# Attention pipeline of an attention and Mamba kernel: eleven-stage order, k's softmax in four exponentials, heads in two banks

## The chip, the cores and the metric

The kernel runs on one core of a Trainium2 chip. The metric is the device time of one execution in microseconds (us), and lower is better. The engines are TensorE (PE, its weight loads are listed apart as PEld), VectorE (DVE), ScalarE (ACT), GpSimd (POOL) and the DMA queues, here issued by SyncE (SP) and by ScalarE.

## What is computed

`x` has 128 sequences of 64 steps and 256 features. A first layer normalises x, makes q, k and v, and does a linear attention with 16 heads of 16 features:

```python
xn = layernorm(x);  q, k, v = xn @ Wq + bq, xn @ Wk + bk, xn @ Wv + bv
k = where(mask, -inf, k);  v = where(mask, 0, v)
q = softmax(q, over the 16 features of a head);  k = softmax(k, over the 64 steps)
attn = einsum('bhse,bhsd->bhed', k, v);  y = einsum('bhtd,bhed->bhte', q, attn)
scale, shift = split(silu(emb) @ film_emb_W + film_emb_b)
x = x + silu(layernorm(y) * (1 + scale) + shift) @ film_out_W + film_out_b
```

A second layer normalises that again, modulates it with the rows of `silu(c) @ W_ada + b_ada`, runs a Mamba scan over the 64 steps and adds the result, gated. `c` and `emb` are the same input `cond`.

## The kernel before

There are two phases, one after the other. **The attention phase** works on 64 tiles of 128 tokens (two sequences of 64 steps in each). It is a software pipeline written out by hand. Every engine has a function `iteration(j, stages)`, which `attention_iterations` calls for j = 0 to 70; work under `if s in stages` is for tile j - s. An engine issues its work strictly in the order of the code, so the order inside `iteration` is the schedule. Between engines there are counting semaphores: `later(eng, S["name"], k)` waits until tile k's step has been done, and `reuse(eng, S["name"], k, slots)` waits until a buffer with so many slots has come free. **The Mamba phase** (`mamba_*`) begins on every engine with `attention_over`, which waits for the last stores of the attention phase. It starts with a gather from the tensor `normed`.

One tile goes through these steps, with the profile's line numbers: VectorE's statistics of x (L1533, L1540), GpSimd's reciprocal root (`rstd`, L1184, L1186), VectorE's normalising (`xn`, L1579), TensorE's turning (L1301), ScalarE's scale and bias out of the bank (`xnT`, L1391), TensorE's products for k (L1283) and for q and v (L1293). VectorE adds bias and mask to k (L1567), takes the maximum over the 64 steps (L1589), subtracts it (L1605), ScalarE takes the exponential of 128x256 at once (L1398), VectorE adds up (L1556) and inverts (L1561), and GpSimd multiplies (L1194). q goes through bias (L1602), maximum (L1608), subtraction (L1617), exponential (L1407), sum (L1553) and reciprocal (L1558). TensorE turns k and q (L1321, L1324), ScalarE copies them (L1403). `heads_product` (L1264) multiplies k by v with 64 rows of the array for each of the two sequences, both into the bank `b_at`; its second half waits for `at_half`, the end of the first, and the product for k (L1283) stands between the halves. VectorE masks the heads (L1584), TensorE makes y (L1311), VectorE scales it (L1612) and takes its statistics; GpSimd normalises it (`yn`, L1174), TensorE turns it (L1345), ScalarE applies four scale and bias columns (L1423) and a tanh (L1427), VectorE finishes the activation (`fs`, L1595), TensorE makes the output product (L1335), VectorE adds x (L1624). x had the output bias added by GpSimd (L1218). GpSimd normalises the sum (`xh`, L1174) and SyncE stores `resid` and `normed`. Further GpSimd work for each tile is the mask row as numbers (`mneg`, L1210).

Once-only work stands at the end of certain iterations: conditioning, film products (L1246, j = 3), and the ada products (L1253 and L1255, at j = 4 and 5 on TensorE into `b_fo_ps`), which VectorE turns into modulation rows (L1518) and a gate row (L1528).

Of the kernel before, what the change touches and what calls it, by code (L numbers as in the profile page):

```python
# [54 lines left out]
STAGES = 8  # L55
# [8 lines left out]
def build(nc, x, cond, itok, mask, norm_scale, norm_bias, Wq, bq, Wk, bk, Wv, bv,  # L64
# [6 lines left out]
    ssm_out = nc.dram_tensor("ssm_out", (BATCH, STEPS, D), F32, kind="Internal").ap()  # L71
    resid_seq = resid.rearrange("(b t) f -> b t f", t=STEPS)
    normed_seq = normed.rearrange("(b t) f -> b t f", t=STEPS)

    with ExitStack() as ctx:  # L75
# [52 lines left out]
        mask_bc = sb("mask_bc", [P, MRING, P], attn_mem, I32)  # L128
# [13 lines left out]
        kmax = sb("kmax", [P, FB * SEQS], attn_mem)  # L142
        ksum = sb("ksum", [P, FB * SEQS], attn_mem)
# [20 lines left out]
        for par in range(2):  # L164
# [17 lines left out]
        bank = [ctx.enter_context(nc.psum_tensor(f"bank{i}", [P, 512], F32)) for i in range(8)]  # L182
        b_xT, b_qvp, b_kT, b_kq, b_at, b_y, b_ynT, b_fo_ps = bank
# [22 lines left out]
        s_mask_f = sem("mask_as_float")  # L206
        s_mask_turned = sem("mask_turned")
# [9 lines left out]
        names = ("x_stats x_meanvar x_rstd x_norm xT_ready xnT_ready qv_ready kT_ready mneg_ready "  # L217
                 "k_biased k_max k_shifted k_exp k_sum k_rec k_normed q_max q_shifted q_exp q_sum q_rec v_ready "
                 "kq_turned kq_ready at_half at_ready at_masked y_ready y_scaled y_stats y_meanvar y_rstd y_norm ynT_ready "
# [17 lines left out]
        def reuse(eng, s, tile, slots):  # L237

            if tile >= slots:
                eng.wait_ge(s, tile + (1 - slots))  # L240

# [849 lines left out]
        def _(sp):  # L1091
            def load(k):

                reuse(sp, S["x1_ready"], k, XRING)
                apart(sp)
                sp.dma_start(xt[:, k % XRING, :], x_tok[k * P:(k + 1) * P, :]).then_inc(s_x[k % XRING], 16)
                reuse(sp, S["mneg_ready"], k, MRING)
                apart(sp)
                sp.dma_start(mask_bc[:, k % MRING, :],
                             mask_flat[k * P:(k + 1) * P].rearrange("(a n) -> a n", a=1).to_broadcast([P, P]))\  # L1100
                    .then_inc(s_mk[k % MRING], 16)
# [24 lines left out]
            weights(s_fo_w, (w_fo[:, :, :], film_out_W))  # L1126
            columns(s_cols_b, (fb_col, film_b), (fns_col, film_norm_scale), (fnb_col, film_norm_bias),
                    (conv_bias, conv_b), (dt_bias, b_dt), (d_col, D_param))

            def iteration(j, stages):  # L1130
                if j > 0 and j + AHEAD < TILES:
                    load(j + AHEAD)
                if 7 in stages:
                    k = j - 7
# [3 lines left out]
                if 6 in stages:  # L1138
                    k = j - 6
# [16 lines left out]
        def _(gp):  # L1156
# [20 lines left out]
            def iteration(j, stages):  # L1177
                done = [n for n, stage in enumerate((1, 5, 7)) if stage in stages]
                if done:
                    p, n = (j - 1) % 2, slice(done[0], done[-1] + 1)  # L1180
                    for norm in done:
                        later(gp, S[("x_meanvar", "y_meanvar", "x1_meanvar")[norm]], j - (1, 5, 7)[norm])
                    apart(gp)
                    gp.tensor_scalar(rstd[:, n, p, 1:2], mv[:, n, p, 1:2], EPS, None, ALU.add).then_inc(S["var_plus"], 1)  # L1184
                    later(gp, S["var_plus"], j - 1)
                    gp.tensor_tensor(rstd[:, n, p, 0:1], rstd[:, n, p, 1:2],  # L1186
                                     half_pow[:, None, :].to_broadcast([P, len(done), 1]), ALU.pow)\
                        .then_inc(S["rstd_ready"], 1)
                    later(gp, S["rstd_ready"], j - 1)
# [6 lines left out]
                if 5 in stages:  # L1196
                    k = j - 5
                    reuse(gp, S["ynT_ready"], k, 1)
                    apart(gp)
                    normalise(yn[:, :], yt[:, :], 1, k % 2, "y_norm")  # L1200
                if 7 in stages:
                    k = j - 7
                    gp.wait_ge(s_xh_out[k % 2], 16 * (k // 2) + 16)
                    apart(gp)
                    normalise(xh[:, k % 2, :], x1[:, k % 2, :], 2, k % 2, "xh_ready")
                if 0 in stages:
                    gp.wait_ge(s_mk[j % MRING], 16 * (j // MRING) + 16)
                    reuse(gp, S["k_biased"], j, MRING)
                    apart(gp)
                    gp.tensor_scalar(mneg[:, j % MRING, :], mask_bc[:, j % MRING, :], 1.0, -1e30,  # L1210
                                     ALU.is_equal, ALU.mult).then_inc(S["mneg_ready"], 1)
                if 2 in stages:
# [5 lines left out]
                    gp.tensor_tensor(x, x, b_fo[:, :], ALU.add).then_inc(S["x_biased"], 1)  # L1218

# [5 lines left out]
        def _(pe):  # L1225
# [14 lines left out]
            def film_products():  # L1240

                pe.wait_ge(s_condT, 1)
                pe.wait_ge(s_film_in, 16)
                for m in range(4):
                    for c in range(KC):
                        mm = pe.matmul(b_ynT[:, m * P:(m + 1) * P], film_w[:, c, m * P:(m + 1) * P], cond_T[:, c, :],  # L1246
# [3 lines left out]
            def ada_products(a, b):  # L1250

                dst = b_fo_ps[:, 0:b - a]
# [7 lines left out]
            def heads_product(k, q):  # L1260

                rows = slice(q * STEPS, (q + 1) * STEPS)
                for h in range(FB):
                    mm = pe.matmul(b_at[:, (q * FB + h) * P:(q * FB + h + 1) * P], vt[rows, k % 4, h * P:(h + 1) * P],  # L1264
# [3 lines left out]
            def iteration(j, stages):  # L1268
                if 4 in stages:
# [4 lines left out]
                    heads_product(k, 0).then_inc(S["at_half"], 1)  # L1274
# [14 lines left out]
                if 2 in stages:  # L1289
                    k = j - 2  # L1290
                    reuse(pe, S["qv_biased"], k, 1)
                    for c in range(FB):
                        mm = pe.matmul(b_qvp[:, :], xnT[:, k % 2, c, :], w_qv[:, c, :],  # L1293
                                       start=(c == 0), stop=(c == FB - 1))
                    mm.then_inc(S["qv_ready"], 1)
                if 1 in stages:
                    k = j - 1
                    later(pe, S["x_norm"], k)
                    reuse(pe, S["xnT_ready"], k, 1)
                    for c in range(FB):  # L1300
                        mm = pe.transpose(b_xT[:, c * P:(c + 1) * P], xn[:, c * P:(c + 1) * P], ident[:, :])  # L1301
                    mm.then_inc(S["xT_ready"], 1)
                if 4 in stages:
                    k = j - 4
                    later(pe, S["at_masked"], k)
                    reuse(pe, S["y_scaled"], k, 1)
                    if k == 0:
                        pe.wait_ge(s_condT, 1)
                    for i in range(4):
# [37 lines left out]
                if j == 1:  # L1347
                    turn_mask()
# [337 lines left out]
```

## Time and profile before

| | |
|---|---|
| runs | 2012.58 us median of 3 (2011.74 to 2015.48) |
| profiled execution, its own time | 2011.82 us |
| its span, first to last instruction | 2010.1 us |
| busy share of the span | PE 94%, DVE 94%, POOL 85%, ACT 82%, PEld 73% |
| attention phase | from the start to 488.2 us, when the last tile's store of `normed` is issued |

In the lists of instructions in order of time a row gives the start in us from the span's start, the length in us, the engine, the line, the operation, output and inputs, the shape and how many instructions it merges. In brackets stands the idle time before it and who ended it. Neighbours on one engine overlap a little, so the distance from start to start is what an instruction costs its engine, and it is less than its length.

### The profile page before, as it was taken

To read this page: it belongs to the slowest core of one execution; us is meant where nothing else is said; L and a number is where in the kernel's file an instruction comes from. 1 tells how busy PE (TensorE), PEld (TensorE's weight loads), DVE (VectorE), ACT (ScalarE), POOL (GpSimd) and SP (SyncE) were. 2 spreads that over 40 slices of the span, in tenths; PEclk is the share of its full clock that TensorE was granted. 3 is DMA by queue.
4 is the path that set the end of the run, shared out by engine and by line. 5 is a ranking of instruction groups with operands and counts; after the bars stand their busy time and mean duration, and the time that the engine had idled before them with its cause. 6 is when DMAs were issued, how large, how long until landed. Compare 5 with 4: busy or idle time off the path is not lost. (4 is left out here: it accounts for less than half of the span.)

```text
span 2010.1 us, 42901 instructions
## 1 busy us (share of the span) xinstructions
PE 1881.6 (94%) x12641; PEld 1463.5 (73%) x12641; DVE 1897.2 (94%) x3750; ACT 1648.6 (82%) x3563; POOL 1701.6 (85%) x1929
## 2 busy tenths in 40 slices
PE   6999999995799999999999999999999999999873
PEld 4666666663378787787878778787878788787773
DVE  5999999995699999999999999999999999999997
ACT  2555655563799999999999999999999999999881
POOL 3788888887289999999999999999999999998582
PEclk9999999997999999999999999999999999999997
DMA  6222222211000000000000000000000000001164
GB/s 169 62 66 65 70 69 66 65 61 58 26 7 11 17 12 12 12 13 11 17 17 12 12 12 12 12 17 6 17 17 12 12 12 12 12 7 48 59 226 183
DMA packets 71401, 80.78 MB, mean 40 GB/s; under 512 B 12227, under 2 KB 63619, under 8 KB 69124
## 3 DMA queue, kind: packets, MB, share of 16 engines
q1 hardware_dynamic: 69024, 70.67, 11.3%
q10 hardware_dynamic: 2148, 7.38, 1.0%
q8 instruction: 105, 1.72, 0.4%
q14 instruction: 124, 1.02, 0.2%
HBM read 44.46 MB, written 33.55 MB: 39 GB/s over the span
## 5 line engine op out<-in xcount | busy, mean ns | idle before, releaser
L814 ACT ACTIVATE decay<-dtT,decay_rate 128x256 f32<-128x256 f32 x2048 | 864.8, 495 | 0.6
L690 PE MATMUL bank<-ident,decay 128*128 128x128 f32 x4096 | 612.9, 273 | 46.5 <-DVE state L951 23.3
L690 PEld LDWEIGHTS bank<-ident,decay 128*128 128x128 f32 x4096 | 477.6, 142 | 105.3 <-ACT decay L814 63.7
L705 PEld LDWEIGHTS bank<-ident,scaled 128*128 128x128 f32 x3496 | 414.5, 141 | 180.9 <-issue 145.7
L705 PE MATMUL bank<-ident,scaled 128*128 128x128 f32 x3496 | 529.1, 274 | 1.9 <-POOL scaled L598 0.2
L951 DVE SCALAR_TENSOR_TENSOR fresh<-dtx,bc,bank 128x512 f32<-128x512 f32 x512 | 357.7, 740 | 0.0
L951 DVE SCALAR_TENSOR_TENSOR state<-dtx,bc,bank 128x512 f32<-128x512 f32 x512 | 357.6, 740 | 0.0
L941 DVE TENSOR_TENSOR bank<-bank,state 128x512 f32<-128x512 f32 x512 | 338.0, 693 | 19.7 <-PE bank L690 14.8
L941 DVE TENSOR_TENSOR bank<-bank,fresh 128x512 f32<-128x512 f32 x512 | 336.4, 692 | 14.0 <-PE bank L690 9.3
L598 POOL TENSOR_SCALAR scaled<-state,bc 128x512 f32<-128x512 f32 x378 | 261.7, 699 | 70.4 <-DVE state L951 44.8
L598 POOL TENSOR_SCALAR scaled<-fresh,bc 128x512 f32<-128x512 f32 x381 | 265.2, 699 | 39.7 <-DVE fresh L951 27.3
L622 POOL TENSOR_TENSOR xs<-xs,tap_bcT 128x512 f32<-128x512 f32 x174 | 222.7, 1280 | 13.4
L603 POOL TENSOR_TENSOR scaled<-scaled 128x512 f32<-128x512 f32 x150 | 192.3, 1282 | 2.5
L1391 ACT ACTIVATE xnT<-bank,col 128x128 f32<-128x128 f32 x128 | 51.7, 454 | 156.5 <-PE bank L1301 156.5
L618 POOL TENSOR_SCALAR tap_bcT<-raw,taps 128x512 f32<-128x512 f32 x174 | 121.7, 699 | 25.6 <-DVE xs L1047 25.2
L1293 PE MATMUL bank<-w_qv,xnT 128*128 128x512 f32 x256 | 127.8, 622 | 0.0
L735 PE MATMUL bank<-w_out,zs 128*128 128x256 f32 x512 | 126.2, 380 | 1.4 <-DVE zs L960 0.9
L747 PE MATMUL bank<-hT,w_in 128*128 128x512 f32 x240 | 122.3, 595 | 1.8 <-ACT hT L825 1.3
L738 PE MATMUL bank<-hT,w_in 128*128 128x512 f32 x240 | 122.9, 594 | 0.0
L860 ACT ACTIVATE scaled<-state,bc 128x512 f32<-128x512 f32 x134 | 95.5, 713 | 24.9 <-DVE state L951 24.8
L860 ACT ACTIVATE scaled<-fresh,bc 128x512 f32<-128x512 f32 x131 | 93.2, 711 | 12.6 <-DVE fresh L951 12.2
L735 PEld LDWEIGHTS bank<-w_out,zs 128*128 128x128 f32 x512 | 89.9, 190 | 10.2 <-issue 1.1
(164 smaller groups left out, 3269.8 us busy)
## 6 DMA issues: line engine op xcount, KB each, us to landing
xt<-in_x_dram SPq DMA_DIRECT2D x64, 128.0 KB, 2.3
resid<-x SPq DMA_DIRECT2D x64, 128.0 KB, 1.7
normed<-xh SPq DMA_DIRECT2D x64, 128.0 KB, 1.7
fin_r<-resid SPq DMA_DIRECT2D x8, 1024.0 KB, 4.9
xg<-normed SPq DMA_DIRECT2D x60, 128.0 KB, 2.1
ssm_out<-yo SPq DMA_DIRECT2D x30, 256.0 KB, 2.1
tap_bcT<-ssm_out SPq DMA_DIRECT2D x44, 128.0 KB, 2.2
mask_bc<-in_mask_BxS_ik_dram SPq DMA_DIRECT2D x64, 64.0 KB, 2.9
```

The source lines that it names most:

```text
L598: gp.tensor_scalar(dst, h, cn, 1.0, ALU.mult, ALU.mult).then_inc(s_scaled_p, 1)
L603: gp.tensor_tensor(scaled[:, i % RING, :], scaled[:, i % RING, :], scaled[:, (i - 1) % RING, :], ALU.add)\
L622: gp.tensor_tensor(x, x, tap[:, :], ALU.add).then_inc(s_tapadd, 1)
L690: mm = pe.transpose(dec_bank[i % DECAY_BANKS][:, m * P:(m + 1) * P], decay[:, i // BLOCK % 2, n % GROUP, m, t % HALF * P:(t % HALF + 1) * ...
L705: mm = pe.matmul(y_bank[t % HALF][:, m * P:(m + 1) * P], scaled[:, i % RING, m * P:(m + 1) * P], ident[:, :], is_transpose=True, start=Fal ...
L735: mm = pe.matmul(side[:, q * D:(q + 1) * D], zs[k % 2][:, m, t * P:(t + 1) * P], w_out[:, m, :], start=(m == 0), stop=(m == CB - 1))
L738: mm = pe.matmul(side[:, :], w_in[:, piece, DI + b * P:DI + (b + 1) * P], hidden(k)[:, piece, :], start=(piece == 0), stop=(piece == FB - 1))
L814: act.activation(decay[:, block % 2, e // CB, m, :], dtT[c % 2][:, m, half * HTOK:(half + 1) * HTOK], ACT.Exp, scale=decay_rate[:, m, n:n ...
L860: act.activation(dst, h, ACT.Copy, scale=cn).then_inc(s_scaled_a, 1)
L941: ve.tensor_tensor(dec_bank[i % DECAY_BANKS][:, :], dec_bank[i % DECAY_BANKS][:, :], h, ALU.mult)\
L951: ve.scalar_tensor_tensor(state_of(n, t), dtx[c % 2][:, t, :], bc[:, c % 2, t, n:n + 1], dec_bank[i % DECAY_BANKS][:, :], ALU.mult, ALU.ad ...
L1293: mm = pe.matmul(b_qvp[:, :], xnT[:, k % 2, c, :], w_qv[:, c, :], start=(c == 0), stop=(c == FB - 1))
```

## The change

The attention pipeline is reordered and regrouped:

- Eleven stages instead of eight. The numbers are now counted apart for each engine: VectorE starts with tile j at j and ends it at j + 6, TensorE uses stages 2 to 7, ScalarE 0 to 4, GpSimd 1 to 9, SyncE up to 10. The order of work in every `iteration` is new.
- k's softmax: VectorE gives the negative maximum. ScalarE takes four exponentials of 128x64, each with the negative maximum as its bias and with a sum as a further output (`accum_out`). VectorE's subtraction and sum of k are gone.
- The two halves of `heads_product` go into two banks (4 and 5) and are issued one behind the other, with no semaphore between them. VectorE masks both in one instruction.
- The turned x and the turned y share one bank (`b_turn`), with waits so that TensorE doesn't write while ScalarE reads.
- The mask as numbers is made once by VectorE, stored to DRAM by ScalarE's queue, and loaded for each tile by broadcast into `mneg`. GpSimd's work on it is gone.
- The ada products move to the end: TensorE's iteration 68, into `b_qvp` and `b_kT`, and VectorE's rows of them to its iteration 67. Film products go into `b_fo_ps`, an iteration later for TensorE.

The diff, cut to its core:

```diff
-STAGES = 8
+STAGES = 11
+X_STAGE, Y_STAGE, X1_STAGE = 1, 5, 8
...
+        low, heads, high = [ps(f"bank{i}", 512) for i in range(4)], ps("bank45", 1024), [ps(f"bank{i}", 512) for i in (6, 7)]
+        b_turn, b_qvp, b_kT, b_kq, _, _, b_y, b_fo_ps = bank
+        b_xT, b_ynT = b_turn[:, 0:D], b_turn[:, D:2 * D]
+        b_at = heads[:, :].rearrange("p (q f) -> p q f", q=SEQS)[:, :, 0:2 * P]
...
         # sync
+            def load_mask(k):
+                reuse(sp, S["k_biased"], k, MRING)
+                sp.dma_start(mneg[:, k % MRING, :], mask_rows[k:k + 1, :].to_broadcast([P, P])).then_inc(s_mk[k % MRING], 16)
+            sp.wait_ge(s_mask_out, 16)
+            for k in range(AHEAD + 1):
+                load_mask(k)
...
         # gpsimd: xh of j-9, k's product of j-3, x's bias of j-2, then rstd for (j-1, j-5, j-8), then yn of j-5
-                if 0 in stages:
-                    gp.tensor_scalar(mneg[:, j % MRING, :], mask_bc[:, j % MRING, :], 1.0, -1e30,
-                                     ALU.is_equal, ALU.mult).then_inc(S["mneg_ready"], 1)
...
         # tensor: q,v product of j-3; turn k,q of j-4; y of j-5; turn y of j-6; turn x of j-2; output of j-7;
         #         both heads products of j-4; k product of j-2
-                    heads_product(k, 0).then_inc(S["at_half"], 1)
+                    heads_product(k, 0)
+                    heads_product(k, 1).then_inc(S["at_ready"], 1)
-                if 4 in stages:
-                    later(pe, S["at_half"], j - 4)
-                    heads_product(j - 4, 1).then_inc(S["at_ready"], 1)
+                if j == TILES + 4:
+                    later(pe, S["qv_biased"], TILES - 1)
+                    ada_products(b_qvp[:, :], 0, 2 * D)
+                    later(pe, S["k_biased"], TILES - 1)
+                    ada_products(b_kT[:, 0:D], 2 * D, 3 * D)
...
         # scalar: exp of q and v of j-2; exp of k of j-1; copy k,q of j-2; xnT of j; film of j-4
+            act.wait_ge(s_mask_f, 2)
+            act.dma_start(mask_rows, mask_row[:, :]).then_inc(s_mask_out, 16)
-                    act.activation(kk, kk, ACT.Exp).then_inc(S["k_exp"], 1)
+                    later(act, S["k_max"], k)
+                    for g in range(FB * SEQS):
+                        kk = kT[:, k % 2, g, :]
+                        ins = act.activation(kk, kk, ACT.Exp, bias=kmax_neg[:, g:g + 1],
+                                             accum_out=ksum[:, k % 2, g:g + 1])
+                    ins.then_inc(S["k_exp"], 1)
...
         # vector: stats of x j; mean of y j-4; shift q j-2; mean of x j; x1 of j-6; bias k j-1; mask heads j-3;
         #         max k j-1; fs j-5; xn j; stats of x1 j-6; sum q j-2; bias qv j-1; 1/sum q j-2; scale y j-3;
         #         max q j-1; 1/sum k j-1; stats of y j-3; mean of x1 j-6
-                    ve.tensor_reduce(ksum[:, :], kT[:, k3 % 2, :, :], AX.X, ALU.add).then_inc(S["k_sum"], 1)
-                    ve.tensor_tensor(kk, kk, kmax[:, :, None].to_broadcast([P, FB * SEQS, STEPS]), ALU.subtract)\
-                        .then_inc(S["k_shifted"], 1)
+                    ve.tensor_reduce(kmax_neg[:, :], kT[:, k1 % 2, :, :], AX.X, ALU.max, negate=True)\
+                        .then_inc(S["k_max"], 1)
-                if j == 4:
-                    clamp_order()
-                    modulation_rows()
-                if j == 5:
-                    mamba_constants()
-                    gate_rows()
+                if j == 6:
+                    clamp_order()
+                if j == 7:
+                    mamba_constants()
+                if j == TILES + 3:
+                    modulation_rows()
+                    gate_rows()
```

The lines that begin with `#` sum up the new order of an engine in words; they are not in the kernel.

## Rows read from the trace of the kernel before

**Rows 1.** The page's first part: busy time and share of each engine.

```profile
PE 1881.6 (94%) x12641; PEld 1463.5 (73%) x12641; DVE 1897.2 (94%) x3750; ACT 1648.6 (82%) x3563; POOL 1701.6 (85%) x1929
```

**Rows 2.** Busy time by stretch: steady part and tail (after the bounds, PE to POOL).

```profile
51.07:454.46 403.39, 396.68 (x2322) 274.86 (x2321) 396.26 (x1276) 239.04 (x638) 328.07 (x405) 1.00 0.22 66
454.46:488.50 34.04, 22.43 (x120) 14.52 (x118) 21.20 (x61) 13.16 (x36) 23.85 (x29) 0.82 0.14 47
```

**Rows 3.** Waits from 100 to 450 us: sum, times, longest.

```profile
PEld bank L1264 <- ACT kq L1403: 17.8, 50, 0.5
```

**Rows 4.** Instructions in order of time: VectorE in one steady iteration.

```profile
251.29 0.41 DVE L1556 TENSOR_REDUCE ksum<-kT 128x4 f32<-128x256 f32 x1
...
251.62 0.24 DVE L1558 RECIPROCAL qrec<-qsum 128x16 f32<-128x16 f32 x1
...
251.85 0.61 DVE L1567 SCALAR_TENSOR_TENSOR kT<-bank,col,mneg 128x128 f32<-128x128 f32 x2
...
252.37 0.42 DVE L1533 BATCH_NORM_STATS2 stats<-xt 128x6 f32<-128x256 f32 x1
...
252.72 0.66 DVE L1579 TENSOR_SCALAR xn<-xt,mv,rstd 128x256 f32<-128x256 f32 x1
...
253.30 0.68 DVE L1584 TENSOR_TENSOR attnT<-bank,head_mask 128x512 f32<-128x512 f32 x1
...
253.90 0.40 DVE L1589 TENSOR_REDUCE kmax<-kT 128x4 f32<-128x256 f32 x1
...
255.22 0.41 DVE L1605 TENSOR_TENSOR kT<-kT,kmax 128x256 f32<-128x256 f32 x1
```

**Rows 5.** In order of time: GpSimd's two-tensor work in that iteration.

```profile
252.62 0.61 POOL L1194 TENSOR_TENSOR kT<-kT,krec 128x256 f32<-128x256 f32 x1
...
256.62 0.73 POOL L1218 TENSOR_TENSOR xt<-xt,b_fo 128x256 f32<-128x256 f32 x1
```

**Rows 6.** In order of time: two encounters of GpSimd and VectorE, at 51 and 464 us.

```profile
50.53 1.23 POOL L1174 TENSOR_SCALAR yn<-yt,mv,rstd 128x256 f32<-128x256 f32 x1
...
51.07 0.40 DVE L1579 TENSOR_SCALAR xn<-xt,mv,rstd 128x256 f32<-128x256 f32 x1
...
464.12 0.73 POOL L1218 TENSOR_TENSOR xt<-xt,b_fo 128x256 f32<-128x256 f32 x1
...
464.35 0.79 DVE L1617 TENSOR_TENSOR qe<-qv,qmax 128x256 f32<-128x256 f32 x1
```

**Rows 7.** In order of time: TensorE and ScalarE groups of the steady iteration.

```profile
250.44 1.27 ACT L1423 ACTIVATE fu<-bank,film_t,film_s 128x64 f32<-128x64 f32 x4
...
254.18 0.66 PE L1311 MATMUL bank<-attnT,kq 128*64 128x128 f32 x8
...
254.28 0.81 ACT L1391 ACTIVATE xnT<-bank,col 128x128 f32<-128x128 f32 x2 [2.12 <-PE bank L1301]
...
255.99 0.58 ACT L1403 ACTIVATE kq<-bank 128x512 f32<-128x512 f32 x1
...
256.62 0.71 PE L1264 MATMUL bank<-kq,vt 64*128 64x128 f32 x4
...
257.26 1.16 PE L1283 MATMUL bank<-xnT,w_k 128*128 128x128 f32 x8
```

**Rows 8.** In order of time: landmarks of the fill, the ada products and the tail.

```profile
17.16 0.61 DVE L1567 SCALAR_TENSOR_TENSOR kT<-bank,col,mneg 128x128 f32<-128x128 f32 x2 [2.58 <-PE bank L1283]
...
35.25 1.12 PE L1253 MATMUL bank<-b_mod,ones_row 1*128 1x512 f32 x2
...
40.04 0.42 DVE L1518 SCALAR_TENSOR_TENSOR mod_scale<-bank,gamma_bc 128x256 f32<-128x256 f32 x1 [1.98 <-PE bank L1255]
...
57.26 0.61 DVE L1567 SCALAR_TENSOR_TENSOR kT<-bank,col,mneg 128x128 f32<-128x128 f32 x2
...
460.62 0.61 DVE L1567 SCALAR_TENSOR_TENSOR kT<-bank,col,mneg 128x128 f32<-128x128 f32 x2
...
488.20 0.34 SPq L1137 DMA_DIRECT2D normed<-xh  x1
```

More of the change, by code:

```diff
@@ L1268, in iteration @@
             def iteration(j, stages):
+                if 3 in stages:
+                    k = j - 3
+                    if k == 0:
+                        pe.wait_ge(s_attn_w, 16 * 5)
+                    later(pe, S["xnT_ready"], k)
+                    reuse(pe, S["qv_biased"], k, 1)
+                    for c in range(FB):
+                        mm = pe.matmul(b_qvp[:, :], xnT[:, k % 2, c, :], w_qv[:, c, :],
+                                       start=(c == 0), stop=(c == FB - 1))
+                    mm.then_inc(S["qv_ready"], 1)
@@ new lines, in iteration @@
+                if 5 in stages:
+                    k = j - 5
+                    later(pe, S["at_masked"], k)
+                    reuse(pe, S["y_scaled"], k, 1)
+                    if k == 0:
+                        pe.wait_ge(s_condT, 1)
+                    for i in range(4):
+                        q, h = i // FB, i % FB
+                        mm = pe.matmul(b_y[q * STEPS:(q + 1) * STEPS, h * P:(h + 1) * P],
+                                       kq[:, k % 2, D + h * P + q * STEPS:D + h * P + (q + 1) * STEPS],
+                                       attnT[:, i, :], start=True, stop=True)
+                    mm.then_inc(S["y_ready"], 1)
@@ new lines, in iteration @@
+                if 2 in stages or 6 in stages:
+                    kx, ky = j - 2, j - 6
+                    if 0 < kx <= TILES:
+                        later(pe, S["xnT_ready"], kx - 1)
+                    if 0 < ky <= TILES:
+                        later(pe, S["film_in"], ky - 1)
+                if 6 in stages:
+                    later(pe, S["y_norm"], ky)
+                    for c in range(FB):
+                        mm = pe.transpose(b_ynT[:, c * P:(c + 1) * P], yn[:, c * P:(c + 1) * P], ident[:, :])
+                    mm.then_inc(S["ynT_ready"], 1)
@@ L1296, in iteration @@
[L1296 to L1309, printed above, removed]
-                        q, h = i // FB, i % FB
-                        mm = pe.matmul(b_y[q * STEPS:(q + 1) * STEPS, h * P:(h + 1) * P],
-                                       kq[:, k % 2, D + h * P + q * STEPS:D + h * P + (q + 1) * STEPS],
-                                       attnT[:, i, :], start=True, stop=True)
-                    mm.then_inc(S["y_ready"], 1)
@@ L1338, in iteration @@
[L1338 to L1347 removed]
+                if j == 2:
```

358 lines of the change are left out of this document (170 added, 188 removed).

## The prediction, made before the result was known

> **What bounds the kernel now.** I read the page's busy shares first [rows 1]: PE and DVE stand equal at 94%, so the average decides nothing. The change touches the attention phase alone, so next I read the busy time by stretch. Between VectorE's normalising of tile 5 (51.07 us) and of tile 63 (454.46 us) the loop is steady: 58 periods in 403.39 us, 6.95 us each, with VectorE busy 396.26 us and TensorE 396.68 us, both 98% [rows 2]. Busy time of PE includes waits inside a matmul's record, so the third view is the list of waits: in 100 to 450 us VectorE has none worth a row, while TensorE's loads wait 0.35 us in each of 50 iterations for ScalarE's copy of k and q, which in turn comes behind VectorE's chain [rows 3]. VectorE's queue is full and sets the period; TensorE is a few tenths behind. The fourth view, instructions in order of time, prices each step from start to start [rows 4 to 8].
>
> **VectorE's period.** Gone are the sum of k, 0.33 us from start to start (251.29 to 251.62), and the subtraction, of the same length 0.41 us, so 0.33 us too [rows 4]. The negated maximum I cost like the maximum, 0.40 us long as before, the same shape. That leaves 6.95 - 0.66 = 6.29 us.
>
> Two encounters with GpSimd move. Today xn lasts 0.66 us (0.58 from start to start), because k's product on GpSimd (two tensors) begins at 252.62, just before it [rows 4, 5]. At 51.07 the same xn lasts 0.40 us though GpSimd's yn has been running since 50.53 [rows 6]. So GpSimd's tensor by tensor work holds up such a VectorE instruction and its scalar work doesn't. In the new order xn comes while GpSimd does yn, so xn costs 0.40 less the usual overlap of 0.08, 0.32 us: 0.26 us less. But k's reciprocal now starts GpSimd's k product, and then x_biased: 0.61 + 0.73 us plus about 0.08 us ahead of each, so x_biased runs from 0.77 to 1.50 us after the reciprocal's end. VectorE meanwhile does two statistics (0.35 each, as 252.37 to 252.72 [rows 4]) and two means (tiny tensors, an estimate of 0.1 each), and comes to q's subtraction, with two tensors in SBUF, about 0.9 us after it. It is caught. The row for that is at 464.35: the same q subtraction, with x_biased on GpSimd since 464.12, took 0.79 us and ended 0.29 us after it [rows 6]. So it ends at 1.79 instead of 1.31: 0.45 us more. VectorE's period: 6.29 - 0.26 + 0.45 = 6.48 us. Bounds: 6.03 us if the two miss each other, 6.55 us if both collisions stay.
>
> The Trainium skill (SBUF — State Buffer, Who interferes with whom) says more: a two-tensor DVE instruction contends with any GpSimd instruction that reads SBUF, and a DVE instruction in a two-port mode and GpSimd block each other for the whole instruction. The trace agrees for 464.35 and disagrees for 51.07, where xn began amid yn and was not held.
>
> **TensorE's period.** Today four heads matmul passes (one half) last 0.71 us and there are two such groups, while y's eight passes in two column halves need 0.66 us together [rows 7], so the column halves run side by side. In two banks the row halves may do so too: one group of some 0.66 instead of 2 x 0.64 us from start to start (256.62 to 257.26), 0.64 us less. One interruption of the full-width products goes as well: k's product takes 1.16 us for eight passes of 128 columns between the halves, against 0.66 for eight in pairs. So 6.95 less 0.64 is at most 6.3 us, and about 6.1 with a further switch saved. If the halves don't overlap, 0.45 us comes back, 6.55 to 6.75 us. I take 6.1 to 6.3: hidden behind VectorE.
>
> The Trainium skill (TensorEngine Tiling (Array Packing), Gotcha 1: PSUM Pressure) says that row tiles write different banks and can't use one bank at once; no row of this trace has row halves in two banks, so it can't be checked yet.
>
> **The four exponentials.** Four activations of 64 columns with column operands take 1.27 us (fu) [rows 7]. The sum's read-out, x us for each, has no row. Below: 0. Above: a whole small activation's slot, 1.27/4 = 0.3 us. I take half, 0.15. ScalarE was busy 239.04/58 = 4.1 us a period [rows 2]; with 1.27 + 0.6 on top, and the single exponential not even taken off, it is 6.0, so its sum is no bound. Its place in the order can be: the loop kmax 0.40, four exponentials 1.27 + 4x, copy of k and q 0.50, xnT 0.81, k's product 1.16 [rows 7], k's bias 0.52 (251.85 to 252.37), masking of heads 0.60 (253.30 to 253.90) [rows 4], and some 0.16 for four handovers. Sum 5.42 + 4x: 6.0 us at 0.15, 6.6 us at 0.3. So at 0.15 it lies hidden behind 6.48; it sets the period from x = 0.27 on.
>
> **GpSimd and the DMAs.** GpSimd loses the mask work (0.66 us in 5.66, 328.07/58 [rows 2]) and stays under the period. SyncE issues the same number of DMAs for a tile. Its queue now waits once for the mask's round trip through DRAM, behind which stand the columns for film; and load_mask(j + 2) waits for VectorE's bias of tile j - 2, with two whole iterations before the data are needed. I cost these at nothing; if the first masks are late, the first k bias moves by 1 to 3 us.
>
> **Steady part.** From k's bias of tile 5 (57.26) to that of tile 63 (460.62) it is 403.4 us [rows 8]. After: 58 x 6.48 = 375.8, and 2.3 us (an estimate, about a dozen short instructions of 0.2) for order table and Mamba constants, which now fall there: 378.1. Gain 25.3 us.
>
> **Fill.** The first k bias was at 17.16, the sixth at 57.26 [rows 8]: 40.1 us. The first x no longer waits behind the second tile's load, so I put the first bias at about 15, 2.1 us earlier (it can't be before k's weights have landed). Out of the 40.1 go the wait for the ada products 1.98 [rows 8], the four modulation instructions (like mod_scale, 0.35 each, 1.4 us), and the 2.3 us just moved: 34.4; the film products stay. The gate's wait and the k work that five filling iterations no longer do (0.66 each, where VectorE doesn't wait anyway) give about another 1.4: 33. Gain 2.1 + 7.1 = 9.2 us, bounds 5 and 12.
>
> **Tail.** From 460.62 to the last store of normed at 488.20: 27.6 us [rows 8]. TensorE waits a lot there and its granted clock is 0.82 on average over 454 to 488 us, i.e. part of it at 1.2 GHz [rows 2]. The ada products now stand there: 4.8 us for the first 512 columns (35.25 to 40.04) [rows 8], half of it for the other 256, 7.2 us together. They stand ahead of the turn of the last y, which TensorE could otherwise do after some 3 us of that wait, so 4.4 us are exposed. Without them I get 21 us for the last tile's chain (k softmax 3.4, k product and turning 2.9, copy and heads 1.4, masking and y 1.5, statistics 1.2, root and yn 2.4, turn and film 2.4, fs, output, x1 and mean 2.8, root, xh and store 2.9). So 25.4 us, gain 2.2 us; bounds 6.6 gained (all hidden) and 0.7 lost (all exposed). They keep TensorE busy, so its clock should not fall before they end.
>
> **Sum.** 25.3 + 9.2 + 2.2 = 36.7 us. The Mamba phase behind 488.2 us starts from the same gather and is unchanged. The profiled execution took 2011.82, the median is 2012.58: 2012.6 - 36.7 = 1975.9, say 1976 us. Own range: period 6.3 to 6.6 and fill and tail bounds, 1960 to 1988.
>
> **Rivals.**
> 1. *The q subtraction misses x_biased.* For it: the margin is only some tenths. Then VectorE needs 6.03 and TensorE's 6.1 to 6.3 sets the period, at 6.2: 58 x 0.28 = 16 us less, 1960 us.
> 2. *GpSimd's yn holds up xn and fs after all, or the heads don't overlap.* xn would wait for yn's end, about 0.3 us in each iteration, period 6.8; serial heads give 6.55 to 6.75. Against the first: the row at 51.07. Time 1976 + 58 x 0.3 = 1993 us. By the skill's rule named above (SBUF — State Buffer), it is what would come out.
> 3. *The exponentials become the bound, slower than before.* Place: ScalarE between kmax and the copy of k and q. If the read-out waits for each activation's end and then takes a full slot, x is near 0.5, and 5.42 + 2.0 = 7.4 us; against before it decides from x = 0.38 (6.95 us). Time 1976 + 58 x 0.94 = 2031 us. Against: the nearest row has four small activations in 1.27 us, so it would have to more than double them.
> 4. *The gain dissolves in new waits* (the longer way of a tile through more stages doesn't pay in the tail, the period stays at 6.9): 2000 to 2012 us. Against: VectorE's queue is full today and two instructions leave it.
>
> **How the numbers follow.** Forecast 0.50, rival 1 0.17, rival 2 0.16, rival 3 0.08, rival 4 0.09 (a third of it within 0.2% of before). From no change this measurement tells about 0.2%, 4 us. Faster: 0.50 + 0.17 + 0.16 + 0.05 = 0.88; same 0.03; slower 0.08 + 0.01 = 0.09. The range takes in rivals 1 and 2 with their spread: 1953 to 1998 us. Out of it lie rivals 3 and 4 and the far end of rival 1.
>
> **What would show it.** Right: a period of VectorE near 6.5 us with 98% busy and no waits; xn at 0.40 us and q's subtraction at 0.8; heads passes in pairs within 0.7 us; the exponentials at 1.3 to 2 us for four; ada products between 430 and 450 us. Wrong: a row in which VectorE waits for TensorE's k product or for heads (ScalarE's chain too long), xn above 0.6 (rival 2), q's subtraction at 0.41 (rival 1), or a fill whose first k bias waits for a mask.

## The result and the profile after

The changed kernel takes 1984.71 us (1982.53 to 1986.35), against 2012.57 us (2011.74 to 2015.48) for the kernel before: ratio 0.9857, 95% interval 0.9845 to 0.9868. That is 28 us less, where 36.7 were forecast; the time lies 9 us above the forecast and inside its range of 1953 to 1998 us. The profiled execution took 1983.11 us, its span 1979.6 us.

First part of the page, of the changed kernel, for [rows 1]:

```profile
PE 1828.8 (92%) x12641; PEld 1424.4 (72%) x12641; DVE 1841.2 (93%) x3623; ACT 1706.3 (86%) x4011; POOL 1659.6 (84%) x1867
```

The landmarks of [rows 8], sixth k bias to last k bias, from there to the last store of `normed`, and the Mamba phase; busy time by stretch, changed kernel:

```profile
52.51:431.28 378.77, 348.79 (x2321) 238.46 (x2320) 347.09 (x1169) 291.50 (x1045) 294.30 (x348) 1.00 0.22 69
431.28:459.77 28.49, 19.24 (x100) 11.29 (x98) 16.46 (x49) 10.49 (x34) 19.77 (x25) 0.94 0.19 61
459.77:1979.50 1519.73, 1426.24 (x10024) 1150.70 (x10024) 1449.25 (x2314) 1381.69 (x2856) 1326.31 (x1458) 0.99 0.09 29
```

The account against the landmarks of before [rows 8]: fill 57.26 to 52.51, 4.8 us less; steady part 403.36 to 378.77, 24.6 us less (6.53 us a period instead of 6.95); tail 27.6 to 28.5, 0.9 us more. Together 28.4 us. The Mamba phase went from 1521.9 to 1519.8 us; in the runs below with the same Mamba phase it is anywhere from 1519 to 1521 us, so I count that as spread.

Two of the 58 periods, the first two, took 8.04 and 7.87 us: the order table and the Mamba constants now fall there. The other 56 have a mean of 6.48 us, exactly the period that was forecast.

The steady figure looks like a hit (25.3 forecast), but the row says something else: VectorE is busy 347 of 379 us, 92%, where I had said 98% and no waits. The waits of the changed kernel, 100 to 430 us (some 50 iterations; sum, times, longest), rows that matter:

```profile
POOL xh L1194 <- issue: 50.9, 47, 1.7
...
PE bank L1327 <- POOL yn L1194: 25.9, 50, 1.2
...
DVE kT L1597 <- PE bank L1360: 22.8, 42, 0.8
```

And those of SyncE's queue in that stretch:

```profile
SPq L240 <- DVE kT L1597: 216.6, 48, 5.1
```

Before, in the same stretch:

```profile
SPq L231 <- POOL xh L1174: 195.6, 48, 4.7
```

SyncE then waited for GpSimd's `xh`, that is for the work that it was to store. Now it stands in `load_mask`, waiting for VectorE's k bias, for 4.5 us in each of 48 iterations. What lies behind that in its queue is seen in order of time, changed kernel, steady part:

```profile
250.00 0.61 DVE L1597 SCALAR_TENSOR_TENSOR kT<-bank,col,mneg 128x128 f32<-128x128 f32 x2 [0.72 <-PE bank L1360]
...
250.70 0.32 SPq L1117 DMA_DIRECT2D mneg<-mask_rows  x1
...
251.13 0.37 SPq L1157 DMA_DIRECT2D normed<-xh  x1
251.33 1.48 POOL L1194 TENSOR_SCALAR yn<-yt,mv,rstd 128x256 f32<-128x256 f32 x1 [0.24 <-POOL rstd L1225]
...
251.79 0.49 DVE L1621 TENSOR_SCALAR xn<-xt,mv,rstd 128x256 f32<-128x256 f32 x1
...
252.25 0.33 ACT L1419 ACTIVATE kT<-kT,kmax_neg 128x64 f32<-128x64 f32 x1
252.49 0.19 ACT L1419 ACTIVATION_READ_ACCUMULATOR kT<-kT,kmax_neg 128x1 f32 x1
252.58 0.33 ACT L1419 ACTIVATE kT<-kT,kmax_neg 128x64 f32<-128x64 f32 x1
...
254.06 1.22 POOL L1194 TENSOR_SCALAR xh<-x,mv,rstd 128x256 f32<-128x256 f32 x1 [1.26 <-issue]
...
255.08 0.38 DVE L1580 TENSOR_TENSOR qe<-qv,qmax 128x256 f32<-128x256 f32 x1
...
255.25 0.69 POOL L1208 TENSOR_TENSOR kT<-kT,krec 128x256 f32<-128x256 f32 x1
...
258.04 1.40 POOL L1194 TENSOR_SCALAR yn<-yt,mv,rstd 128x256 f32<-128x256 f32 x1 [0.24 <-POOL rstd L1225]
...
259.58 0.41 PE L1327 MATMUL bank<-ident,yn 128*128 128x128 f32 x2 [0.64 <-POOL yn L1194]
...
261.00 0.72 PE L1279 MATMUL bank<-kq,vt 64*128 64x128 f32 x8
...
262.86 0.61 DVE L1597 SCALAR_TENSOR_TENSOR kT<-bank,col,mneg 128x128 f32<-128x128 f32 x2 [0.71 <-PE bank L1360]
```

Read it as one loop. The k bias (250.00 to 250.61) lets the mask load go (250.70), and only behind that stands the store of `normed` (251.13). Such a store takes 2.8 us to land (median), and GpSimd's next `xh` needs the landing of a store, since there are two `xh` buffers; it begins 1.26 us late here (254.06). The profile names no releaser for that wait ("issue"); that it is the store is read from the code and from 251.13 + 2.8 = 253.9, and tested with e1 and e6. It makes GpSimd late with k's product, x's bias, `rstd` and `yn` (258.04). TensorE stands 0.64 us before the turn of y (259.58), behind which are queued the heads (261.00) and the product for k, and for that VectorE's k bias waits 0.71 us (262.86). Two iterations, 12.9 us.

Three things are also to be seen here. The exponentials start 0.33 us apart, and the read of the sum (0.19 us) lies almost wholly under its neighbours. The eight heads passes, both halves, need 0.72 us. And q's subtraction lasts 0.38 us.

### The profile page after: what moved, and what is told of

Read it like the earlier page. It is cut to its first block and busy times, and to the rows that moved or that the text cites. A ratio compares the mean times of both kernels' runs of the same rounds, so it can differ in the third digit from the quotient of the medians.

```text
span 1979.6 us, 43161 instructions
## 1 busy us (share of the span) xinstructions
PE 1828.8 (92%) x12641; PEld 1424.4 (72%) x12641; DVE 1841.2 (93%) x3623; ACT 1706.3 (86%) x4011; POOL 1659.6 (84%) x1867
## 3 DMA queue, kind: packets, MB, share of 16 engines
q14 instruction: 125, 1.02, 0.2%
## 5 line engine op out<-in xcount | busy, mean ns | idle before, releaser
L1419 ACT ACTIVATE kT<-kT,kmax_neg 128x64 f32<-128x64 f32 x256 | 85.8, 336 | 74.5 <-DVE kmax_neg L1610 74.5
L633 POOL TENSOR_SCALAR tap_bcT<-raw,taps 128x512 f32<-128x512 f32 x174 | 120.9, 695 | 25.0 <-DVE xs L1062 24.6
L1194 POOL TENSOR_SCALAR xh<-x,mv,rstd 128x256 f32<-128x256 f32 x64 | 78.4, 1225 | 57.2 <-issue 55.1
L1291 PE MATMUL bank<-w_qv,xnT 128*128 128x512 f32 x256 | 122.5, 601 | 0.0
L1194 POOL TENSOR_SCALAR yn<-yt,mv,rstd 128x256 f32<-128x256 f32 x64 | 90.7, 1417 | 15.2 <-POOL rstd L1225 15.2
```

The lines of the kernel that those rows point to most:

```text
L1194: gp.tensor_scalar(dst, src, mv[:, norm, slot, 0:1], rstd[:, norm, slot, 0:1], ALU.subtract, ALU.mult).then_inc(S[done], 1)
```

## Experiments

Each kernel below is the changed one with one or more edits, but for e8, which is the kernel before with one part of the change. Period is from the sixth to the last k bias, over 58. The kernel before was measured again beside each group of runs, with medians from 2010.85 to 2013.72 us, so differences of medians between kernels of different groups are good to some 3 us; the ratios allow for it. Where kernels are compared by a wait over 100 to 430 us, I use the mean without the first two periods: 6.48 us for the changed kernel, 6.25 in e1, 6.73 in e2, 6.72 in e11, 6.71 in e10.

| kernel | ratio to before, 95% | median, us | period | tail | first and sixth k bias |
|---|---|---|---|---|---|
| changed | 0.9857 (0.9845 to 0.9868) | 1984.71 | 6.53 | 28.5 | 18.47, 52.51 |
| e1, six mask buffers | 0.9795 (0.9778 to 0.9811) | 1970.78 | 6.30 | 28.5 | 19.06, 54.93 |
| e6, stores first | 0.9786 (0.9770 to 0.9803) | 1969.95 | 6.31 | 29.0 | 19.41, 53.56 |
| e7, e1 and x's bias last | 0.9773 (0.9756 to 0.9789) | 1966.94 | 6.25 | 28.5 | 18.93, 52.54 |
| e9, e7 and e5 | 0.9767 (0.9751 to 0.9784) | 1964.64 | 6.25 | 28.4 | 16.73, 52.66 |
| e5, ada weights late | 0.9859 (0.9842 to 0.9875) | 1982.93 | 6.59 | 29.0 | 16.95, 50.43 |
| e4, ada products last | 0.9870 (0.9854 to 0.9887) | 1986.78 | 6.56 | 25.4 | 18.70, 53.86 |
| e3, serial heads | 0.9999 (0.9986 to 1.0012) | 2011.75 | 6.95 | 28.4 | 19.11, 56.34 |
| e10, e1 and serial heads | 0.9946 (0.9926 to 0.9965) | 1999.22 | 6.74 | 28.4 | 18.94, 56.36 |
| e2, one exponential | 0.9950 (0.9933 to 0.9966) | 2001.91 | 6.79 | 29.3 | 17.77, 54.26 |
| e11, e1 and one exponential | 0.9947 (0.9931 to 0.9964) | 1999.31 | 6.78 | 29.3 | 18.46, 54.47 |
| e8, four exponentials in the kernel before | 1.0087 (1.0070 to 1.0104) | 2029.64 | 7.26 | 28.8 | 16.65, 57.40 |

### SyncE's queue: e1 and e6

e1:

```diff
-MRING = 4
+MRING = 6
```

> Changed kernel with six mask slots instead of four, nothing else. Theory Q (SyncE's queue): the steady period of 6.53 us is set by a loop over two iterations: VectorE's bias of k releases the mask load, behind which the store of xh stands in SyncE's queue; the store frees xh's buffer, GpSimd normalises into it, then does k's product, x's bias, the root and yn, and only then TensorE can turn y and x, make k's product, and the next but one bias follows (12.86 us from 250.00 to 262.86). With six slots the mask load waits for a bias two tiles older, so the store goes out early: GpSimd's xh has no wait, the period falls below 6.45 us, the time to 1955 to 1978 us. Since GpSimd then runs early, x_biased should meet q's subtraction, which takes 0.7 to 0.8 us instead of 0.39. Rival P (TensorE's k product comes late for its own reasons, ScalarE's exponentials first): no change, 1982 to 1987 us. Rival V (VectorE's own work is the bound): no change either.

e6 leaves the ring at four buffers and issues the mask's load behind the two stores:

```diff
                     load(j + AHEAD)
-                    load_mask(j + AHEAD)
                 if 10 in stages:
...
                     sp.dma_start(resid[k * P:(k + 1) * P, :], x1[:, k % 2, :]).then_inc(s_x1_out[k % 2], 16)
+                if j > 0 and j + AHEAD < TILES:
+                    load_mask(j + AHEAD)
```

> Changed kernel with four mask slots as it was, but in SyncE's iteration the mask load stands behind the two stores instead of ahead of them. Theory Q (the store stuck behind the mask load's wait is what costs): the same gain as with six slots, 1969 to 1973 us, and GpSimd's xh without the wait. Rival: six slots gained because masks arrived late at VectorE; then this edit, which makes them later still, gains nothing or loses, 1985 us or more.

Both take about 14 us off (13.9 and 14.8 by the medians, 12.5 and 14.3 by the ratios) and bring the period to 6.30. SyncE's queue of e1, 100 to 430 us:

```profile
SPq L240 <- DVE x L1589: 235.5, 54, 5.7
```

It now waits for nothing but VectorE's sum `x`, which the store of `resid` is to take, and GpSimd's wait before `xh` is gone from the list. Since e6 has the same gain with the old ring, it was not masks coming late but the stores standing behind a wait that isn't theirs.

One part of e1's expectation did not come. x's bias and q's subtraction do meet now, but VectorE isn't the one held:

```profile
250.55 1.03 POOL L1216 TENSOR_TENSOR xt<-xt,b_fo 128x256 f32<-128x256 f32 x1
250.60 0.39 DVE L1580 TENSOR_TENSOR qe<-qv,qmax 128x256 f32<-128x256 f32 x1
```

q's subtraction keeps its 0.39 us, where 0.7 to 0.8 were expected, and x's bias takes 1.03 instead of 0.73 us. More on it in the last section.

What is left at 6.30 is in e1's waits, 100 to 430 us:

```profile
POOL kT L1208 <- DVE krec L1650: 29.8, 28, 1.1
...
DVE kT L1597 <- PE bank L1360: 18.5, 26, 0.9
...
PE bank L1327 <- POOL yn L1194: 15.4, 27, 0.8
```

VectorE's and TensorE's come in every second iteration (start to start 5.94 and 6.54 us in turn). Without its wait VectorE would need 6.25 - 18.5/52.8 = 5.90 us, TensorE without its own 5.96: neither is full. That three engines hold each other in a loop is my reading of these waits, not shown by a run.

### GpSimd's order: e7

x's bias moves from before `rstd` to behind `yn` in GpSimd's iteration, on top of e1:

```diff
-                if 2 in stages:
...
-                    gp.tensor_tensor(x, x, b_fo[:, :], ALU.add).then_inc(S["x_biased"], 1)
...
                     normalise(yn[:, :], yt[:, :], 1, norm_slot(1, k), "y_norm")
+                if 2 in stages:
...
+                    gp.tensor_tensor(x, x, b_fo[:, :], ALU.add).then_inc(S["x_biased"], 1)
```

> Six mask slots, and GpSimd adds the output bias to x (x_biased) after yn instead of before the root. With six slots the periods alternate 5.94 and 6.54 us. Theory G: what is left is again a loop over two iterations, from VectorE's reciprocal of k through GpSimd's k product, x_biased (0.7 to 1.0 us), root and yn to TensorE's turns and k product; taking x_biased out of it makes it 0.7 to 1.0 us shorter for two iterations, and VectorE's own 5.94 us becomes the period: 58 x 0.36 = 21 us less than with six slots alone, 1950 us; at least 10 us less if q's subtraction now collides. Rival P (TensorE's sum with its copies from ScalarE is the bound): no change against six slots alone, 1969 to 1972 us.

It gives some 4 us at most (0.9773 against 0.9795, the intervals overlap), period 6.25, far from the 21 or at least 10 us of the first expectation. TensorE's wait for `yn` becomes rarer (20 instead of 27 times), but GpSimd then waits for VectorE's statistics. So GpSimd's length before `yn` is not what holds the loop at 6.3. What does is open.

### Heads in one or two waves: e3 and e10

Two banks as in the change, but the second half waits for the first:

```diff
-                    heads_product(k, 0)
+                    heads_product(k, 0).then_inc(S["at_half"], 1)
+                    later(pe, S["at_half"], k)
                     heads_product(k, 1).then_inc(S["at_ready"], 1)
```

> Changed kernel in which the second heads half waits for the end of the first, both in their own banks. The heads group becomes 0.65 us longer (0.43 us of passes and a drain). Theory Q: TensorE's heads stand in the two-iteration loop once, so a period gets 0.3 us longer: 12 to 20 us more, 1997 to 2005 us. Rival P: heads stand right ahead of k's product in each iteration, 0.65 us in each period, 38 us more, 2022 us. Rival V: no change.

The whole gain is gone: 27 us more than the changed kernel, period 6.95. That is between the two expectations (1997 to 2005 and 2022 us), and two readings were left: TensorE's own queue, or the loop through SyncE made longer. e10 is e3 with six mask buffers.

> Six mask buffers, and the second half of the heads waits for the end of the first (still two banks). Theory of the engine: the serial halves cost TensorE's own queue some 0.65 us an iteration, whatever the SyncE queue does; its sum of about 6.2 becomes 6.8 to 6.95, and the time is 2000 to 2010 us. Rival, theory of the loop: in the changed kernel the serial halves cost 27 us because they lengthened a loop that runs through the store and the mask's load; without that queue only a part comes back, period 6.4 to 6.6, 1977 to 1990 us.

1999 us, 28 us above e1: the engine, not the loop. TensorE and VectorE of e10 in order of time:

```profile
250.59 1.48 PE L1279 MATMUL bank<-kq,vt 64*128 64x128 f32 x8
...
251.44 1.03 POOL L1216 TENSOR_TENSOR xt<-xt,b_fo 128x256 f32<-128x256 f32 x1
251.48 0.39 DVE L1581 TENSOR_TENSOR qe<-qv,qmax 128x256 f32<-128x256 f32 x1
...
251.99 1.16 PE L1361 MATMUL bank<-xnT,w_k 128*128 128x128 f32 x8
...
253.19 0.61 DVE L1598 SCALAR_TENSOR_TENSOR kT<-bank,col,mneg 128x128 f32<-128x128 f32 x2 [0.91 <-PE bank L1361]
```

The same eight passes in the same two banks take 1.48 us instead of 0.72. In TensorE's list no wait on another engine is left, only its own 0.25 us between the halves, and VectorE waits 0.91 us for the product for k. So this kernel is bound by TensorE, at 6.7 us.

The Trainium skill (TensorEngine Tiling (Array Packing), Gotcha 1: PSUM Pressure) says that row tiles need different banks to run together. What can be seen here agrees: in two banks 0.72 us, in one bank [rows 7] two waves of 0.71. No run here let two row halves into one bank at once.

### k's softmax: e2, e11 and e8

e2 takes k's softmax back to one exponential with VectorE's subtraction and sum, in the new order:

```diff
...
-                    for g in range(FB * SEQS):
-                        kk = kT[:, k % 2, g, :]
-                        ins = act.activation(kk, kk, ACT.Exp, bias=kmax_neg[:, g:g + 1],
-                                             accum_out=ksum[:, k % 2, g:g + 1])
...
+                    act.activation(kk, kk, ACT.Exp).then_inc(S["k_exp"], 1)
...
         # vector
+                    ve.tensor_tensor(kk, kk, kmax_neg[:, :, None].to_broadcast([P, FB * SEQS, STEPS]), ALU.add)\
+                        .then_inc(S["k_shifted"], 1)
...
+                    ve.tensor_reduce(ksum[:, k1 % 2, :], kT[:, k1 % 2, :, :], AX.X, ALU.add).then_inc(S["k_sum"], 1)
```

> Changed kernel with k's softmax as before: subtraction and sum on VectorE, one exponential of 128x256 on ScalarE; order and banks as changed. Theory Q: VectorE has some 0.6 us of waiting in a period, so 0.66 us more work on it costs little: period 6.55 to 6.75, time 1985 to 1998 us. Rival V (VectorE bound): 58 x 0.66 = 38 us more, 2023 us. Rival P (the exponentials' chain is the bound): it gets faster, 1960 to 1980 us.

e11 is e2 with six mask buffers.

> Six mask buffers, and k's softmax as before (VectorE subtracts and adds up, ScalarE takes one exponential). Theory: with the store's wait gone VectorE's sum sets the period in both forms, so the two instructions of 0.33 us are paid in full: 6.30 + 0.66 = 6.96, but less the waits that VectorE still has at 6.30 (some 0.3), so 6.6 to 6.75 and 1988 to 1997 us. Rival: ScalarE's shorter way (one exponential instead of four) gives back more than half of it, period 6.45, 1980 us.

e2 costs 17 us over the changed kernel and e11 28 us over e1, both more than expected, with one and the same period, 6.79 and 6.78. In both VectorE's waits add up to 0.3 us at most from 100 to 430 us, so its own sum sets the period, 6.72 us without the first two. e1's 5.90 and 0.66 make 6.56. I put the remaining 0.16 down to collisions with GpSimd: in both the medians of `xn` and of q's subtraction are 0.56 and 0.59 us, against 0.41 and 0.39 in e1. That alone would be 0.35, so the sum doesn't close. With a full VectorE the queue of SyncE has no effect.

e8 is the same part of the change put alone into the kernel before.

> The kernel before with k's softmax alone changed (negated maximum, four exponentials with sums, no subtraction or sum on VectorE); eight stages, its order, its one heads bank. Theory: VectorE falls from 6.95 to 6.29 us a period, but TensorE, which waited only 0.35 us in a period, then sets it: period 6.6 to 6.9 us, time 1992 to 2009 us. Rival V (VectorE was the only bound, as the step in the prediction says): 6.3 us, 1975 us.

It makes that kernel slower, by 17 us, although two of VectorE's instructions leave; both expectations had it faster. Order of time, e8:

```profile
250.70 0.34 ACT L1400 ACTIVATE kT<-kT,kmax_neg 128x64 f32<-128x64 f32 x1
...
251.04 0.58 ACT L1407 ACTIVATE kq<-bank 128x512 f32<-128x512 f32 x1
251.06 0.42 DVE L1623 TENSOR_TENSOR x<-bank,xt 128x256 f32<-128x256 f32 x1 [0.42 <-PE bank L1335]
251.67 0.52 PEld L1264 LDWEIGHTS bank<-kq,vt 64*128 64x128 f32 x4 [0.67 <-ACT kq L1407]
251.67 0.71 PE L1264 MATMUL bank<-kq,vt 64*128 64x128 f32 x4 [0.43 <-ACT kq L1407]
...
253.50 0.61 DVE L1568 SCALAR_TENSOR_TENSOR kT<-bank,col,mneg 128x128 f32<-128x128 f32 x2 [0.34 <-PE bank L1283]
```

Four exponentials at 0.33 us stand ahead of the copy of k and q. TensorE's loads wait 0.67 us for that copy, where they waited 0.35 before [rows 3], and VectorE now waits for TensorE twice, 0.42 and 0.34 us. The period is 7.26 us.

No run has the new order with both the heads and the softmax as before, so what the order is worth by itself stays open.

### Start and end: e5, e9 and e4

e5 and e9 take the large `ada_w` load and three rows with it from the start to ScalarE's iteration 12:

```diff
...
+                if j == 12:
+                    load_ada_weights()
```

> Changed kernel in which the 1.5 MB of ada weights (with their bias, gamma and beta) are loaded at ScalarE's iteration 12 instead of 0. In the changed kernel the mask's store took 6.9 us to land, the first mask load went out at 12.71 and VectorE waited for it until 18.47 us, with the DMA engines full from 10 to 20 us. Theory: the weights' stream delays mask store and load; without it the first k bias comes at about 15 us and the time falls by 3 to 4 us, 1981 us. Rival: the delay is the queue of first weights (1 MB for q, k, v, output) and the order in SyncE's queue, so the first k bias stays past 17.5 us and the time at 1984 to 1986 us.

> The changed kernel with three edits together: six mask buffers, x's output bias last in GpSimd's iteration, and the load of the ada weights moved from the start to ScalarE's iteration 12. If the three act on separate places (the store's wait in the loop, GpSimd's order, the first mask's way at the start) they add up: 1966.9 less about 1.5 to 2 us, 1965 us. Rival: the late load disturbs the loop at iteration 12 as much as it saves at the start, 1967 us or above.

In the changed kernel's fill the masks are late:

```profile
12.12 2.08 PE L1360 MATMUL bank<-xnT,w_k 128*128 128x128 f32 x8 [3.27 <-DMA b_qv<-in_L_cond_bv_dram]
...
12.71 1.27 SPq L1117 DMA_DIRECT2D mneg<-mask_rows  x3
...
18.47 0.61 DVE L1597 SCALAR_TENSOR_TENSOR kT<-bank,col,mneg 128x128 f32<-128x128 f32 x2 [5.26 <-DMA mneg<-mask_rows]
```

The product for k was done at 14.2 us and the first k bias began at 18.47, at the end of a wait for the mask. With the load moved it begins 1.5 us earlier in e5 and 2.2 us earlier in e9 than in e7, still at the end of a wait for the mask, of 5.0 and 4.0 us. In e9 nothing of it is left at the sixth k bias (52.66 against 52.54 in e7), and though its 1964.6 us are what was expected, its ratio can't be told from e7's. In e5 the sixth is 2.1 us earlier too, but its steady part is longer and the ratio is that of the changed kernel; the 1982.9 us lie between its two expectations. So the first mask's delay is real, but taking 1.5 to 2.2 us from it brings at the end nothing that these runs can tell.

e4 puts the ada products behind all tiles (TensorE's iteration 70, VectorE's rows at 69) and lets the Mamba phase wait for the rows:

```diff
-                if j == TILES + 4:
+                if j == TILES + 6:
 ...
         def attention_over(eng):
+            eng.wait_ge(s_mod, 4)
```

> Changed kernel in which the ada products come after the last output product on TensorE (iteration 70) and the modulation rows at VectorE's last iteration; every engine waits for them before the Mamba phase. The turn of the last y then no longer waits 4.4 us behind them. If the theory of the tail holds and the products hide behind the last store and the gather: 4 us less, 1980.5 us. If they run at half clock or are exposed ahead of the gather: no change to 3 us more.

The tail shrinks by 3.1 us, but the Mamba phase takes 1525.8 us instead of 1519.8, and the ratio, 0.9870, can't be told from the changed kernel's. The products in the changed kernel, in order of time:

```profile
445.42 3.70 PE L1270 MATMUL bank<-ada_w,cond_T 128*128 128x512 f32 x8
445.62 0.42 DVE L1556 BATCH_NORM_STATS2 stats<-x 128x6 f32<-128x256 f32 x1
445.78 1.23 POOL L1194 TENSOR_SCALAR yn<-yt,mv,rstd 128x256 f32<-128x256 f32 x1 [0.24 <-POOL rstd L1225]
...
451.50 0.38 PE L1327 MATMUL bank<-ident,yn 128*128 128x128 f32 x2
...
454.17 1.13 PE L1342 MATMUL bank<-w_fo,fs 128*128 128x256 f32 x4 [1.42 <-DVE fs L1615]
```

and in e4:

```profile
456.20 1.06 PE L1269 MATMUL bank<-b_mod,ones_row 1*128 1x512 f32 x1
457.18 6.09 PE L1271 MATMUL bank<-ada_w,cond_T 128*128 128x512 f32 x8
463.20 0.69 PE L1269 MATMUL bank<-b_mod,ones_row 1*128 1x256 f32 x2
```

In the changed kernel the last `yn` ended at 447.0 and its turn started at 451.50: 4.5 us exposed, as forecast (4.4). But there the products run at the 2.4 GHz level (granted clock 1.00 from 445.4 to 450.4 us), 3.70 us for the large one, and the output product behind them takes 1.13 us; the last two in the tail of the kernel before took 2.07 and 2.08 us. From the last k bias to the last store the mean granted clock is 0.94, against 0.79 before (460.62 to 488.20 us). In e4 TensorE comes to the products out of the waits of the tail, the mean granted clock is 0.78 in the tail and 0.72 in the 15 us behind it, and the large product takes 6.09 us. So moving the work out of the way gained nothing. Which part of the 6.0 us in the Mamba phase is the lower clock and which the wait of every engine for the rows, this run doesn't separate.

## Why the prediction came out as it did

The time was inside the range and the direction right, but two of the steps behind the steady part were wrong and hid each other.

**VectorE's queue sets the period.** This step failed for the changed kernel: VectorE's own sum is 6.48 - 22.8/50.9 = 6.03 us and it waits 0.45 us a period, where I had said none. In the kernel before it has no wait, so there the step may stand, but e8 shows a second limit close behind: with 0.66 us taken from VectorE and some 0.9 us added to ScalarE ahead of its copy, the period grows by 0.31. How close it was, e8 can't tell, since it changes both. I had read the 0.35 us of waits in [rows 3] as slack; they were the sign of that second limit.

**The two encounters.** The first went as forecast, though not wholly: `xn` lasts 0.46 us on average during `yn` (0.66 before, 0.40 forecast). The second did not come: q's subtraction takes 0.40 on average, not 0.8, and 0.45 us of the sum did not exist. In the changed kernel GpSimd is late because `xh` waits, and x's bias begins after the subtraction. So the two miss each other, as in rival 1, and its 6.03 us is what VectorE needs; but rival 1 had TensorE set the period at 6.2. And where the two do meet, in e1, it is GpSimd that pays. The upper bound of this term was also summed wrongly: 6.29 us already holds the first collision, so both together make 6.29 + 0.45 = 6.74, not 6.55.

**GpSimd and the DMAs cost nothing.** This step failed. I priced the data (two iterations early) and the round trip, and wrote down myself that `load_mask` waits for VectorE's bias, but not what is queued behind it: the store of `normed`, whose landing frees GpSimd's buffer. It costs 14 us (e1, e6), 0.23 us a period. So the period of 6.48 is right by chance: 0.45 us for a collision that did not come, and 0.45 us of waits that I did not foresee. Without the queue's part the period is 6.25 (e1); what holds the rest is not settled.

**TensorE, hidden at 6.1 to 6.3.** Its own sum is about 6.0 us. The serial value, 6.55 to 6.75, is right too (6.74 in e10). But I called the saving hidden, and without it 27 us come back (e3), against 17 without the new softmax (e2). With six mask buffers each of the two is worth 28 us (e10, e11): neither hides the other.

**The exponentials.** Each costs 0.33 us start to start; the four of `fu`, without a sum, lasted 1.27 us, 0.32 each [rows 7]. So x is some 0.02 us, not 0.15, and rival 3 was far off in this order. In the order of before it would have been right in sign: e8 is slower.

**Fill.** Forecast 9.2 us, came 4.8. From the first to the sixth k bias it is 34.0 us (forecast 33), but the first came at 18.5, not 15: the mask, for which I had named 1 to 3 us and counted none. e9 says that removing part of that wait doesn't carry through, so its price at the end stays open between 0 and 3.5 us.

**Tail.** Forecast 2.2 us less, came 0.9 more. The exposed 4.4 us were right. The last tile's chain without them was sized at 21 us and is 24: from the last k bias to the end of the last `yn` it took 15.7 us, where my terms add up to 12.8. That it is because the last tile passes through more stages behind other tiles' work, which I had priced as if it ran alone, no run tests.

Of 36.7 us forecast and 28.4 found, the fill lacks 4.4, the tail 3.1 and the steady part 0.7. The steady part's 0.7 is the once-only work: the first two periods take 3.0 us above the mean of the others, where 2.3 was estimated.

## What to carry to other kernels

For each wait that a change adds to an in-order queue, write down what stands behind it and who waits for that, DMA queues included; issuing the waiting transfer behind the stores was worth 14 us here, as much as two more buffers. Two engines at 98% are two limits: taking work from one and lengthening the other's chain can lose (e8), and a part of a change that loses alone can be worth much together with another (the four exponentials: 17 us lost in e8, 17 and 28 gained by e2 and e11). A period that comes out right proves nothing until its waits do.

The best version of these is e9, 1964.6 us: 18 us (0.9%) under the changed kernel by the ratios 0.9767 and 0.9857, some two thirds of it e1's one number.

## What the runs showed of the hardware

When GpSimd and VectorE both work tensor by tensor, it isn't always VectorE that pays; in these traces it goes with the distance of their starts. At 464.35 in the kernel before VectorE's subtraction started 0.23 us after GpSimd's x bias and was stretched to 0.79 us [rows 6]. In e2, from 60 to 430 us, q's subtraction starts 0.3 us after GpSimd's k product some 50 times; it takes 0.59 or 0.60 us, and the k product its normal 0.61. In e1 it starts at most 0.06 us after x's bias some 50 times; there it takes 0.38 to 0.40 us, and x's bias 1.02 to 1.04 instead of 0.73 us. e10 repeats that as often (251.44 and 251.48 above).

The Trainium skill (SBUF — State Buffer, Who interferes with whom) says that the order of issue decides who is held. That such a pair contends, the rows agree with; but in e1 and e10 the one whose record starts first is the one held, so the order of the records' starts doesn't tell it. The same section of the Trainium skill lists VectorE's tensor-with-scalar operation among those that can run in a two-port mode and then block, or be blocked, for a whole instruction; outside such a mode an instruction with one SBUF input doesn't contend. The prediction took the row at 51.07 as disagreeing with this. It need not: `xn` takes 0.40 us there, no less than q's subtraction of the same shape (0.39), so nothing here shows that it runs in a two-port mode. In the changed kernel `xn` during `yn` takes 0.46 us on average (`yn` 1.44, where its shortest is 1.23): stretched a little, not blocked.

The read of the accumulator after an activation is an instruction of its own of 0.19 us, almost wholly under the next one.
